# A fused decoder layer on one core: opening and closing written out, another standing order, gates as column tiles, three steps of each batch's negations on GpSimd

## Chip, cores and metric

One Trainium2 chip, one core. The metric is the device time of one execution in microseconds (us); the figure of a kernel is the median of its runs.

## What is computed

Sixteen independent batches of 256 rows by 256 columns in float32 go through one decoder layer:

```python
# per batch b, x[b] and ctx[b] are 256 x 256
x = layernorm(x + attn(x))                 # 16 heads of 16, scores + bias(|i-j|), softmax, Wo
x = layernorm(x + mlstm(x, ctx, ctx))      # 4 heads of 64: gates, cumulative sums, D matrix, head norm
x = layernorm(x + ffn(x))                  # 256 -> 1024 -> 256, rows quantised, weights ternary

# inside mlstm
ig = [q, ctx, ctx] @ igate_kernel + igate_bias          # 4 columns, fg alike
cs = cumsum(log_sigmoid(fg)); log_D = cs_i - cs_j + ig_j; m = max_j log_D
C = (q k^T / 8) * exp(log_D - m);  h = C v / (max(|sum C|, exp(-m)) + 1e-6)

# inside ffn
xq = round(x * 127 / max|row|);  wq = clip(round(w / mean|w|), -1, 1)
```

## The kernel before, in words

The work is written engine by engine. Each of the five blocks (SP for the DMAs, GpSimd, TensorE, ScalarE, VectorE) has a set of small functions, one for each step of a batch, and a function body(b) that calls them in an order written by hand. body(b) mixes four ages of batches: the projections of batch b+2, the attention of b and b+1, the memory part (gates, D matrix, values) of b-1 and b-2, and the feed-forward part of b-2 and b-3. body is called for b = -2 to B+3, and a step whose batch does not exist is left out (live). So the first and the last batches go through the same order as the middle ones, with holes.

Data passes between engines through semaphores. Each step waits until its inputs stand and until its output buffer is free, and an instruction that waits holds everything behind it on its engine.

For a group of the attention ("head" or step s), TensorE makes the scores (L599) into pS, VectorE adds the bias and takes the row maximum (L1292, two row tiles), ScalarE forms mx - score for row tile 0 (negated, L935) and GpSimd for tile 1 (negated, L437), TensorE transposes both tiles (turned, L615), ScalarE takes the exponential (L947), and TensorE multiplies four heads by their values in one call of values (L632). sc, pr and mx are rings of 8 heads.

The memory part: TensorE makes the gates in mem_gates with four matmuls that accumulate into one bank (L761 for the context, L764 for x1, 68 columns of which 8 are used). ScalarE reads them (L986 to L990), then takes the logarithm (L997, with a table load). VectorE sums (forget_sums, L1552), adds (input_rows, L1560), takes the running maximum (running_max, L1568), and a DMA writes this to DRAM (save_max, L319) and another one spreads it over all partitions (spread_max, L326). ScalarE takes its exponentials (mem_late, L966; mem_weights, L974), GpSimd masks (mem_causal, L489), VectorE multiplies (mem_weights, L1542), and TensorE makes the values (mem_values, L739 to L741).

The feed-forward part: rows are scaled on ScalarE (quantised, L1047), rounded back on VectorE (quantised_rows, L1467), turned on TensorE, multiplied (L693, L706), gated on VectorE, scaled on ScalarE (scaled, L1124), rounded back on GpSimd (inner_quantised, L449), turned by a DMA (turn_inner, L337), multiplied again (down, L751) and added to the residual (ffn_residual, L1532).

q and k are split into three bfloat16 parts on GpSimd (split_high and split_low, L414 to L427), and twelve DMAs of 128 KB a batch stack them (load_stack, L299).

All smaller products of TensorE share three PSUM banks, pA, pB and pC. The list uses fixes which name has which bank, by its place in the list modulo 3, and lease finds from the list whose release must be waited for. apart puts a semaphore increment of its own in front of some instructions.

Before the first body with scores stands a setup. All four attention weights are loaded and turned, the three bias vectors are spread by matmuls with a row of ones, the whole attention bias (4 MB) is loaded, and the three feed-forward weights are averaged (L1256), rounded (L1206, L1264, L1265) and turned on TensorE (L914) ahead of the iterations.

## Time and profile before

| | us |
|---|---|
| median of 3 runs | 768.72 |
| lowest and highest | 763.31 and 770.01 |
| the profiled execution, device time | 766.44 |
| its span in the profile | 764.6 |

The profile covers one execution. The span runs from its first to its last instruction; the device time is 1.8 us more. PE is TensorE's matmuls, PEld its weight loads, DVE VectorE, ACT ScalarE, POOL GpSimd, and SPq the queue of SP that issues the DMAs.

### The profile page before, as it was taken

To read this page: it belongs to the slowest core of one execution; us is meant where nothing else is said; L and a number is where in the kernel's file an instruction comes from. 1 tells how busy PE (TensorE), PEld (TensorE's weight loads), DVE (VectorE), ACT (ScalarE), POOL (GpSimd) and SP (SyncE) were. 2 spreads that over 40 slices of the span, in tenths; PEclk is the share of its full clock that TensorE was granted. 3 is DMA by queue.
4 is the path that set the end of the run, shared out by engine and by line. 5 is a ranking of instruction groups with operands and counts; after the bars stand their busy time and mean duration, and the time that the engine had idled before them with its cause. 6 is when DMAs were issued, how large, how long until landed. Compare 5 with 4: busy or idle time off the path is not lost.

```text
span 764.6 us, 17069 instructions
## 1 busy us (share of the span) xinstructions
PE 640.8 (84%) x4882; PEld 476.4 (62%) x4912; DVE 617.4 (81%) x2261; ACT 597.5 (78%) x1253; POOL 483.2 (63%) x833
## 2 busy tenths in 40 slices
PE   4367997999999999999999999989999989785542
PEld 3345776667676758686868676867676757452311
DVE  2755464899999999999999999988999999875752
ACT  0415795999999998989898999988999989875421
POOL 2415654667777868787778777776777765535332
PEclk8587998999999999999999999999999999897855
DMA  8887624154445545454545453635353542120201
GB/s 266 156 143 111 97 60 74 23 114 65 123 74 112 83 113 84 111 84 112 84 111 84 109 87 89 95 85 101 70 117 60 108 59 72 42 56 15 69 15 41
DMA packets 96966, 68.32 MB, mean 89 GB/s; under 512 B 40229, under 2 KB 96618, under 8 KB 96874
## 3 DMA queue, kind: packets, MB, share of 16 engines
q1 hardware_dynamic: 96874, 67.23, 44.7%
q8 instruction: 41, 0.67, 0.4%
q14 instruction: 51, 0.42, 0.2%
HBM read 29.39 MB, written 4.26 MB: 44 GB/s over the span
## 4 chain that ended last, share of the span: by engine, by line
PE 28%; DMA 23%; ACT 13%; SPq 10%; DVE 10%; issue 10%; POOL 6%; POOLq 0%; ACTq 0%; DVEq 0%
DMA mb<-mrows 13%; DMA th<-hq 7%; SPq L299 6%; PE pT L615 3%; PE pO L632 3%; ACT L997 2%; PE pA L751 2%; ACT h L1124 2%; SPq L337 2%; DVE mm L1568 2%; PE pB L739 2%; DMA ks<-parts 2%; PE pB L764 1%; PE pB L761 1%; PE pS L599 1%
## 5 line engine op out<-in xcount | busy, mean ns | idle before, releaser
L1292 DVE CUSTOM_DVE_ANT_0 sc<-pS,bias 128x256 f32<-128x256 f32 x512 | 201.4, 416 | 28.0 <-PE pS L599 26.8
L947 ACT ACTIVATE pr<-pT 128x512 f32<-128x512 f32 x256 | 154.5, 608 | 22.0 <-PE pT L615 21.4
L615 PE MATMUL pT<-ident,sc 128*128 128x128 f32 x1024 | 153.1, 277 | 5.1 <-POOL sc L437 3.2
L437 POOL TENSOR_SCALAR sc<-sc,mx 128x256 f32<-128x256 f32 x256 | 123.3, 493 | 23.3 <-DVE mx L1292 20.8
L615 PEld LDWEIGHTS pT<-ident,sc 128*128 128x128 f32 x1024 | 119.6, 142 | 28.1 <-issue 17.1
L935 ACT ACTIVATE sc<-sc,mx 128x256 f32<-128x256 f32 x256 | 130.2, 516 | 3.0 <-DVE mx L1292 3.0
L599 PE MATMUL pS<-ks,qs 96*128 96x256 bf16 x512 | 93.8, 274 | 9.1 <-DVE mx L1292 6.5
L489 POOL TENSOR_SCALAR_AFFINE_SELECT mb<-mb 128x256 f32<-128x256 f32 x64 | 26.3, 411 | 80.2 <-ACT mb L974 79.2
L632 PE MATMUL pO<-pr,va 128*32 128x256 f32 x1024 | 70.2, 393 | 0.5 <-ACT pr L947 0.5
L599 PEld LDWEIGHTS pS<-ks,qs 96*128 96x128 bf16 x512 | 47.9, 98 | 34.0 <-DVE mx L1292 17.0
L449 POOL TENSOR_SCALAR hq<-h 128x512 bf16<-128x512 f32 x64 | 38.7, 620 | 32.0 <-ACT h L1124 31.8
L414 POOL TENSOR_SCALAR parts<-qk_f 128x512 bf16<-128x512 f32 x32 | 19.9, 621 | 56.0 <-ACT qk_f L1092 39.1
L751 PE MATMUL pA<-wd,th 128*128 128x256 bf16 x256 | 37.4, 295 | 19.4 <-DMA th<-hq 17.8
L1036 ACT ACTIVATE x<-y,shift,rs 128x256 f32<-128x256 f32 x64 | 34.7, 592 | 20.3 <-POOL shift L402 20.3
L632 PEld LDWEIGHTS pO<-pr,va 128*32 128x32 f32 x1024 | 27.1, 110 | 29.8 <-issue 9.7
L1488 DVE TENSOR_TENSOR h<-h,pA 128x512 f32<-128x512 f32 x64 | 43.7, 683 | 1.1 <-PE pA L706 0.7
L1304 DVE BATCH_NORM_STATS2 st<-y 128x6 f32<-128x256 f32 x96 | 36.0, 417 | 9.4 <-POOL y L505 9.3
L751 PEld LDWEIGHTS pA<-wd,th 128*128 128x128 bf16 x256 | 25.4, 104 | 28.9 <-issue 22.6
L1124 ACT ACTIVATE h<-h,magic,hs 128x1024 f32<-128x1024 f32 x32 | 39.5, 1236 | 4.6 <-DVE hs L1521 4.6
L391 POOL TENSOR_SCALAR ve<-mv 128x2 f32<-128x2 f32 x48 | 12.2, 254 | 48.7 <-DVE mv L1314 48.5
L416 POOL TENSOR_TENSOR qk_f<-qk_f,parts 128x512 f32<-128x512 f32 x32 | 41.2, 1287 | 2.7
L1292 DVE DVE_READ_ACCUMULATOR2_ANT mx<- 128x1 f32 x512 | 41.5, 81 | 0.0
(223 smaller groups left out, 1736.3 us busy)
## 6 DMA issues: line engine op xcount, KB each, us to landing
qs<-parts SPq DMA_DIRECT2D x96, 128.0 KB, 4.7
ks<-parts SPq DMA_DIRECT2D x96, 128.0 KB, 4.5
mb<-mrows SPq DMA_DIRECT2D x16, 512.0 KB, 7.5
xin<-in_x SPq DMA_DIRECT2D x16, 256.0 KB, 2.8
bias<-in_L_attn_pos_bias SPq DMA_DIRECT2D x4, 1024.0 KB, 20.8
xb<-in_x SPq DMA_DIRECT2D x16, 256.0 KB, 3.0
cx<-in_ctx SPq DMA_DIRECT2D x32, 128.0 KB, 2.1
out<-hq SPq DMA_DIRECT2D x16, 256.0 KB, 3.2
```

Source lines behind the costliest of these rows:

```text
L299: sp.dma_start(dst, src).then_inc(stack.sem, 16)
L416: pool.tensor_tensor(src, src, parts[:, 0, which, :, :], ALU.subtract).then_inc(split.sem, 1)
L437: pool.tensor_scalar(sc[:, s % RING, 1, :], sc[:, s % RING, 1, :], -1.0, mx[:, s % RING, 1:2], ALU.mult, ALU.add).then_inc(neg_g.sem, 1)
L599: ins = pe.matmul(pS[s % 2][:, t * S:t * S + S], qs[par][:, s, t * P:t * P + P], ks[par][:, s, :], start=True, stop=True)
L615: ins = pe.transpose(bank[:, kt * S + t * P:kt * S + t * P + P], sc[:, s % RING, t, kt * P:kt * P + P], ident[:])
L632: ins = pe.matmul(pO[32 * j:32 * j + 32, 0:S], va[par][:, kt, hd, :], pr[:, hd % RING, kt, :], start=(kt == 0), stop=(kt == TT - 1))
L751: ins = pe.matmul(bank[:, 0:D], hqT[:, t, j, :], wd[:, j, :], start=(j == 0), stop=(j == FT - 1))
L935: act.activation(sc[:, s % RING, 0, :], sc[:, s % RING, 0, :], ACT.Identity, bias=mx[:, s % RING, 0:1], scale=-1.0).then_inc(neg_a.sem, 1)
L947: act.activation(flat(pr[:, s % RING, :, :]), pT[s % 2][:, :], ACT.Exp, scale=-1.0)\
L1124: act.activation(h[:, t, :], h[:, t, :], ACT.Identity, bias=magic[:, :], scale=hs[:, 4, t:t + 1])\
L1292: dve.tensor_tensor_reduce(out=sc[:, s % RING, t, :], in0=pS[s % 2][:, t * S:t * S + S], in1=bias[:, t, s, ::-1], scale=1.0, scalar=LOW, o ...
L1488: dve.tensor_tensor(dst, dst, bank_of(f"u{i}")[:, :], ALU.mult).then_inc(h_v.sem, 1)
```

## The change

- The bodies are called for batches 4 to 11 alone. opening() and closing() stand in each engine's block as lists of calls, each list with an order of its own, and body(b) has another order too.
- lease no longer reads a list of uses. TensorE's calls are counted as the program is built: each lease takes the next of the three banks and waits for the release, found in the table freed, of what held that bank. y0 and y1 of a batch had one bank and now have two.
- The setup is part of the opening. Loads have the order Wq, x[0], Wk, bq and bk, a quarter of the bias, Wv, x[1], the next quarter, Wo, the three spread bias vectors (by DMA), w_gate. The bias tile holds 384 columns for each head and the two row tiles read overlapping windows of it, 3 MB in place of 4. The feed-forward weights go one at a time through the tile h, and are turned by DMAs instead of TensorE. Their steps on ScalarE and VectorE lie between steps of batches 0 and 1, those of w_gate ahead of the first scores.
- k of batch 0 is split on VectorE.
- Gates: gate_parts makes four matmuls into four column tiles of 32, ScalarE copies the result (gate_copy), and gate_sums adds the four by one matmul with a matrix fold of zeros and ones.
- In heads 2, 7 and 12 of each batch GpSimd forms both row tiles of the negation, and ScalarE none.
- quantised_rows and input_rows go from VectorE to GpSimd.
- apart is gone.

```diff
+POOL_HEADS = (2, 7, 12)
-        bias = sb("bias", [P, TT, NH, S])
+        bias = sb("bias", [P, NH, S + P])
...
         def lease(eng, name, batch):
 
-            n = names.index(name)
...
+            if len(leases) >= len(shared):
+                other, n = leases[-len(shared)]
+                signal, k = freed[other]
+                eng.wait_ge(signal.sem, signal.at(n, k))
+            banks[name, batch] = shared[len(leases) % len(shared)]
+            leases.append((name, batch))
+            return banks[name, batch]
...
+            def gate_parts(c):
...
+                for j in range(4):
+                    rows = cxT if j < KT else x1T
+                    ins = pe.matmul(bank[32 * j:32 * j + 32, 0:S], gate_w[:, 2 + j if j < KT else j - KT, :],
+                                    rows[:, j % KT, :], start=True, stop=True)
+                ins.then_inc(gp_ps.sem, 1)
...
+                bank = lease(pe, "gates", c)
+                pe.wait_ge(gp_sb.sem, gp_sb.at(c, 1))
+                pe.matmul(bank[0:64 + XH, 0:S], fold[:, :], gt[:, :], start=True, stop=True).then_inc(gt_ps.sem, 1)
...
+            def weight_turn(i):
+                sp.wait_ge(wt_v.sem, 2 * i + 2)
...
+                sp.dma_start_transpose(dst, tern[i]).then_inc(d_wt[i].sem, 16)
...
-                pool.tensor_scalar(sc[:, s % RING, 1, :], sc[:, s % RING, 1, :], -1.0, mx[:, s % RING, 1:2],
-                                   ALU.mult, ALU.add).then_inc(neg_g.sem, 1)
+                for t in range(TT) if s in POOL_HEADS else (1,):
+                    ins = pool.tensor_scalar(sc[:, s % RING, t, :], sc[:, s % RING, t, :], -1.0, mx[:, s % RING, t:t + 1],
+                                             ALU.mult, ALU.add)
+                ins.then_inc(neg_g.sem, 1)
...
+                pool.tensor_scalar(xq[:], xr[:], 1.0, -MAGIC, ALU.mult, ALU.add).then_inc(xq_g.sem, 1)
...
+                pool.tensor_tensor(am[z, :], gt[z, :], cs[:, :], ALU.add).then_inc(am_g.sem, 1)
...
+            opening()
+            for b in range(FIRST, LAST):
+                body(b)
+            closing()
```

How the order moves, at three places. First TensorE in a middle batch, around the gates, before (L751 is down for row tile 1, L761 and L764 are the gates, L599 scores, L615 a transpose, L648 the projections of q and k, pS to pC the banks):

```order
L751 MATMUL pA<-wd,th 128x256 x8
L599 MATMUL pS<-ks,qs 128x256 x2
L615 MATMUL pT<-ident,sc 128x128 x4
L761 MATMUL pB<-cxT,gate_w 68x256 x2
L764 MATMUL pB<-x1T,gate_w 68x256 x2
L599 MATMUL pS<-ks,qs 128x256 x4
L648 MATMUL pC<-xT,wqT 128x256 x4
L599 MATMUL pS<-ks,qs 128x256 x2
L615 MATMUL pT<-ident,sc 128x128 x8
L585 MATMUL pA<-ident_b,xq 128x128 x4
L648 MATMUL pB<-xT,wkT 128x256 x4
L599 MATMUL pS<-ks,qs 128x256 x4
```

And in the changed kernel (L456 down, L470 gate_parts, L274 the transpose of x of batch b+2, L480 gate_sums, L290 scores, L308 transposes, L341 q and k):

```order
L456 MATMUL pB<-wd,th 128x256 x8
L470 MATMUL pC<-cxT,gate_w 32x256 x2
L470 MATMUL pC<-x1T,gate_w 32x256 x2
L274 MATMUL pA<-ident,xin 128x128 x4
L480 MATMUL pB<-gt,fold 68x256
L290 MATMUL pS<-ks,qs 128x256 x4
L308 MATMUL pT<-ident,sc 128x128 x8
L341 MATMUL pC<-xT,wqT 128x256 x4
L308 MATMUL pT<-ident,sc 128x128 x4
L290 MATMUL pS<-ks,qs 128x256 x2
L341 MATMUL pA<-xT,wkT 128x256 x4
```

The two pairs of gate matmuls become four narrow ones and a sum, with the transpose of x between them. The transposes of three heads, in place of two, stand between the gates and the projection of k, and the transpose of the quantised rows has moved behind k.

Second the DMAs of SP for a middle batch, before (L337 turns the quantised inner rows, L299 stacks q or k, L319 and L326 write and spread the running maximum, L342 stores, L312 loads the context, L305 and L331 load x):

```order
L337 DMA_TRANSPOSE th<-hq 128x8x128
L299 DMA ks<-parts 16x8x512 x6
L337 DMA_TRANSPOSE th<-hq 128x8x128
L319 DMA mrows<-mm 4x256
L305 DMA xin<-in_x 128x2x256
L331 DMA xb<-in_x 128x2x256
L326 DMA mb<-mrows 128x4x256
L299 DMA qs<-parts 16x8x512 x6
L342 DMA out<-hq 128x2x256
L312 DMA cx<-in_ctx 128x256 x2
```

And in the changed kernel (L1263 turns the inner rows, L1225 stacks, L1245 and L1252 write and spread the maximum, L1268 stores):

```order
L1263 DMA_TRANSPOSE th<-hq 128x8x128
L1231 DMA xin<-in_x 128x2x256
L1263 DMA_TRANSPOSE th<-hq 128x8x128
L1225 DMA ks<-parts 16x8x512 x6
L1245 DMA mrows<-mm 4x256
L1257 DMA xb<-in_x 128x2x256
L1252 DMA mb<-mrows 128x4x256
L1268 DMA out<-hq 128x2x256
L1225 DMA qs<-parts 16x8x512 x6
L1238 DMA cx<-in_ctx 128x256 x2
```

The six DMAs that stack k stood between the two transposes of a batch and now stand behind both. The load of x has gone from between the write and the spread of the maximum to between the two transposes.

Third the beginning of TensorE, before up to the first scores (L568 turns the attention weights, L573 to L578 spread the bias vectors, L902 averages and L914 turns the feed-forward weights, L672 is the projection of v):

```order
L578 MATMUL pT<-cxT,hq 128x1 x4
L585 MATMUL pA<-ident,xin 128x128 x4
L648 MATMUL pC<-xT,wqT 128x256 x4
L648 MATMUL pB<-xT,wkT 128x256 x4
L902 MATMUL pT<-w_abs,cxT 128x3
L914 MATMUL pO<-ident_b,h 128x128 x8
...
L585 MATMUL pA<-ident,xin 128x128 x4
L672 MATMUL pC<-wvT,xT 128x256 x4
L648 MATMUL pC<-xT,wqT 128x256 x4
L648 MATMUL pB<-xT,wkT 128x256 x4
L599 MATMUL pS<-ks,qs 128x256 x12
```

And in the changed kernel (L256 turns the attention weights, L266 averages w_gate, L369 is v, L290 the scores):

```order
L274 MATMUL pA<-ident,xin 128x128 x4
L256 MATMUL pS<-ident,pr 128x128 x4
L341 MATMUL pB<-xT,wqT 128x256 x4
...
L341 MATMUL pC<-xT,wkT 128x256 x4
L266 MATMUL pA<-w_abs,cx 64x1 x2
L256 MATMUL pT<-ident,pr 128x128 x2
L274 MATMUL pB<-ident,xin 128x128 x4
L256 MATMUL pT<-ident,pr 128x128 x2
L369 MATMUL pC<-wvT,xT 128x256 x4
L341 MATMUL pA<-xT,wqT 128x256 x4
L341 MATMUL pB<-xT,wkT 128x256 x4
L290 MATMUL pS<-ks,qs 128x256 x6
```

The transposes of the feed-forward weights and the spreading of bias vectors have left TensorE, v of batch 0 has moved ahead of q and k of batch 1, and the average of w_gate has stayed ahead of the first scores.

## Rows read from the trace of the kernel before

**Rows 1.** The page, part 1: busy time, share and instructions of each engine

```profile
PE 640.8 (84%) x4882; PEld 476.4 (62%) x4912; DVE 617.4 (81%) x2261; ACT 597.5 (78%) x1253; POOL 483.2 (63%) x833
```

**Rows 2.** Stretches between the first scores, gates 0, 2, 12, 15 and the end

```profile
core 0: us, PE busy (x) PEld busy (x) DVE busy (x) ACT busy (x) POOL busy (x), PEclk, DMA share, GB/s
0.00:54.90 54.90, 25.77 (x128) 21.71 (x129) 28.93 (x38) 11.41 (x14) 13.83 (x25) 0.75 0.90 197
54.90:103.40 48.50, 41.67 (x312) 31.44 (x313) 25.25 (x127) 32.22 (x71) 30.34 (x50) 0.89 0.56 82
103.40:184.20 80.80, 72.22 (x567) 55.65 (x567) 60.73 (x247) 67.34 (x147) 49.98 (x82) 0.96 0.42 80
184.20:582.00 397.80, 376.33 (x3003) 285.12 (x3022) 367.95 (x1391) 366.22 (x780) 298.13 (x511) 1.00 0.48 94
582.00:698.40 116.40, 99.38 (x767) 70.32 (x770) 98.82 (x363) 96.30 (x202) 71.94 (x131) 0.96 0.28 62
698.40:764.60 66.20, 25.48 (x112) 12.12 (x114) 35.75 (x96) 24.00 (x42) 18.95 (x37) 0.64 0.15 36
```

**Rows 3.** Timeline, 0 to 60 us (start, us, engine, line; idle before in brackets)

```profile
9.16 0.81 DVE L1234 COPY hq<-th 1x256 f32<-1x256 f32 x2 [9.16 <-DMA gate_b<-in_L_xattn_fgate_bias]
...
21.08 4.61 DVE L1256 TENSOR_REDUCE w_abs<-sc 128x1 f32<-128x2048 f32 x2
...
22.99 3.78 PE L648 MATMUL pC<-xT,wqT 128*128 128x256 f32 x8 [0.77 <-ACT xT L1083]
...
31.81 7.31 SPq L299 DMA_DIRECT2D qs<-parts  x6
...
32.45 2.01 POOL L416 TENSOR_TENSOR qk_f<-qk_f,parts 128x512 f32<-128x512 f32 x1
...
54.90 0.61 PE L599 MATMUL pS<-ks,qs 96*128 96x256 bf16 x4 [0.31 <-DMA ks<-parts]
```

**Rows 4.** The chain that ended last, 262 to 302 us (start, us, what)

```profile
269.24 0.99 DVE mm L1568
...
271.62 8.16 DMA mb<-mrows
...
282.19 0.46 PE pA L739 x2
...
290.85 0.59 SPq L299
...
294.75 5.27 DMA th<-hq
```

**Rows 5.** Timeline of TensorE, middle batches (181 to 190 and 262 to 302 us)

```profile
182.40 1.03 PE L761 MATMUL pB<-cxT,gate_w 128*68 128x256 f32 x4
...
184.12 0.60 PE L599 MATMUL pS<-ks,qs 96*128 96x256 bf16 x4
...
270.47 1.07 PE L632 MATMUL pO<-pr,va 128*32 128x256 f32 x16
271.47 0.66 PE L615 MATMUL pT<-ident,sc 128*128 128x128 f32 x4
...
282.19 0.46 PE L739 MATMUL pA<-cx,cT 128*128 128x128 f32 x2 [1.30 <-DVE cT L1542]
```

**Rows 6.** Groups of instructions, 262.45 to 421.32 us, four batches (busy us, mean ns)

```profile
L935 ACT ACTIVATE sc<-sc,mx 128x256 f32<-128x256 f32 x64 | 32.8, 519 | 0.0
L957 ACT ACTIVATE oT<-pO 128x256 f32<-128x256 f32 x16 | 6.3, 392 | 1.2 <-PE pO L632 1.2
L437 POOL TENSOR_SCALAR sc<-sc,mx 128x256 f32<-128x256 f32 x64 | 30.9, 494 | 1.9 <-DVE mx L1292 1.1
L1292 DVE CUSTOM_DVE_ANT_0 sc<-pS,bias 128x256 f32<-128x256 f32 x129 | 51.3, 415 | 1.0 <-PE pS L599 0.5
L1467 DVE TENSOR_SCALAR xq<-att 128x512 bf16<-128x512 f32 x4 | 2.6, 662 | 0.6 <-ACT att L1047 0.4
L1560 DVE TENSOR_TENSOR am<-gt,cs 4x256 f32<-4x256 f32 x4 | 1.6, 412 | 0.1
```

More of the change, by code:

```diff
@@ L224, in lease @@
         def lease(eng, name, batch):
-            n = names.index(name)
-            it = batch + uses[n][1]
-            for back in range(1, 2 * len(uses)):
-                i, m = (it, n - back) if back <= n else (it - 1, n - back + len(uses))
-                if m < 0:
-                    break
-                other, behind, freed, k = uses[m]
-                if bank_of(other) is bank_of(name) and live(i - behind):
-                    wait(eng, freed, i - behind, k)
-                    break
@@ L608, in turned @@
                 bank = pT[s % 2]
-                pe.wait_ge(neg_a.sem, lin + 1)
+                act_heads = s + 1 - sum(h <= s for h in POOL_HEADS)
+                if s not in POOL_HEADS:
+                    pe.wait_ge(neg_a.sem, neg_a.at(b, act_heads))
                 pe.wait_ge(neg_g.sem, lin + 1)
@@ new lines, in body @@
+                down(e, 0)
+                turned(b, 5)
+                v_proj(n)
+                scores(b, 10, par)
+                x1_turned(c, 1 - par)
+                down(e, 1)
+                gate_parts(c)
+                x_turned(n2, par)
+                gate_sums(c)
+                scores(b, 11, par)
+                scores(b, 12, par)
+                turned(b, 6)
+                turned(b, 7)
+                q_proj(n2)
+                turned(b, 8)
+                scores(b, 13, par)
@@ L917, in _ @@
-            pe.wait_ge(v_set.sem, V_ALL)
-            iterations(pe, body)
+                mem_scores(c, 0)
+                scores(n, 5, 1 - par)
+                turned(b, 14)
+                turned(b, 15)
+                mem_values(c, 0)
+                mem_scores(c, 1)
+                scores(n, 6, 1 - par)
+                mem_values(c, 1)
+                values(b, 3, par)
+                mem_values(c, 2)
+                heads_turned(b, 0)
+                heads_turned(b, 1)
+                turned(n, 0)
@@ L1211, in _ @@
+            act.wait_ge(g_set.sem, G_ALL)
+            opening()
+            for b in range(FIRST, LAST):
+                body(b)
+            closing()
         @block.vector
@@ L1706 @@
+            opening()
+            for b in range(FIRST, LAST):
+                body(b)
+            closing()
 _INS = ["x", "ctx_1024", "L0_attn_Wq", "L0_attn_bq", "L0_attn_Wk", "L0_attn_bk", "L0_attn_Wv", "L0_attn_bv",
```

3340 lines of the change are left out of this document (2749 added, 591 removed).

## The prediction

> **What bounds the kernel now.** I read the busy shares first, then the stretches, then the chain of waits, then TensorE's timeline. The shares name no single bound: TensorE 84%, VectorE 81%, ScalarE 78%, GpSimd 63% [rows 1]. The stretches show why. I cut the span at the first scores (54.9 us) and where the gates of batches 0, 2, 12 and 15 end [rows 2]. To the first scores go 54.9 us with TensorE busy for 25.8. From gates 2 to gates 12 ten batches take 397.8, so 39.8 each, and in each TensorE is busy 37.6, VectorE 36.8, ScalarE 36.6, GpSimd 29.8. The last three batches take 38.8 each, and behind gates 15 come 66.2 us in which no engine is busy for more than 54%: a chain of latencies. So there are three prices: the start, the batch, the end.
>
> In a middle batch three engines have 2 to 3 us of air each, and no more than one loop of waits fits in. The chain [rows 4] shows that loop: gates, running maximum at 269.24, the DMA that spreads it (8.16 us), values of the memory at 282.19; then the inner rows, whose turning DMA takes 5.27 and stands behind six issues of k's stack at 0.59 (some 3.8 us with gaps), then down and the next gates. TensorE's own row shows the price: it stood 1.30 us in front of the values, for cT [rows 5]. Relieving one engine by 1 us therefore gives 1 us at most, and only if the loop gets shorter too.
>
> **The batch.** Gates: from 182.40 to the scores at 184.12 TensorE spent 1.72 us on the four products of L761 and L764 with 256 columns, 0.43 each [rows 5]. Four heads' values, eight products in column tiles 32 wide, took 270.47 to 271.47, 1.00, so four such take 0.50. With gate_sums (0.43) the new gates cost 0.93 and save 0.79. In the 1.00 us a switch of tile width is already contained: eight products at 0.43, four at a time, would be 0.86. If the 0.14 belongs to each visit and not to each product, gate_parts costs 0.57, and the saving is 0.72. The Trainium skill has the rule behind this (TensorEngine Tiling (Array Packing), Key Properties: "Mode switching requires drain"); by it the change adds one such visit a batch, and the sum is 0.07 us a batch worse, 1 us in all. The row agrees in size.
>
> ScalarE: three negations at 0.519 leave, the copy of the gates (shape of L957, 0.392) comes: 1.17 less; records of ScalarE overlap, so I count 1.0 [rows 6]. VectorE: 0.662 and 0.412 leave, 1.07 less [rows 6]. GpSimd: three negations at 0.494, quantised_rows and input_rows come. Neither has a row on GpSimd. The first has 512 columns, so it lies between one L437 and two, 0.49 to 0.99; the second has 256 columns on 4 partitions, from 0 (if only partitions counted) to 0.49. I take 0.65 and 0.4: 2.5 more, 32.3 in a batch. The removed apart increments have no row. They take nothing at least, and on VectorE, with 16 a batch, at most its 3 us of idle time [rows 2]; that time is explained by waits, so I count nothing.
>
> So work per batch becomes TensorE 36.8, VectorE 35.7, ScalarE 35.6, GpSimd 32.3. Keeping the air of before (2.2, 3.0, 3.2) gives 38.7 to 39.0.
>
> The order says whether the loop allows it. From the end of the gates (184.12, or 263.4 in the batch of rows 4) to the memory's values at 282.19 went 18.8 us, with 15.7 of work on TensorE. In the new order this stretch holds two more scores (0.22 each), two more heads' transposes (0.44) and one more call of values (1.00): 18.0. Its chain grows as well: one exponential ahead of the logarithm (about 0.5, as L935), four VectorE tiles ahead of the running maximum (0.415 in the record and some 0.35 from start to start, 1.4), one tanh between the two exponentials of the mask (0.5) [rows 6]. The step on GpSimd lies beside the four tiles, and the load of x leaves the place in front of the spread (0.4 less). Some 2.1 in all, so 20.9 to 21.2. The other stretch, values to gates, loses these 2.3 and the gates' 0.8 from its 21.0: 17.9. Its DMA wait should go, because k's stack no longer stands between the two turnings, 3.8 us of slack for the second. Sum 38.8 to 39.1. With the 38.7 to 39.0 above I take 38.8, 1.0 less than now. From gates 2 to 12: 10.0 us gained. For the last three intervals, 38.8 now and bound more by latency, I take half, 0.6 each: 1.8.
>
> New waits in this order: gate_sums waits for ScalarE's copy, with 0.44 of transposes as cover; the copy's 0.39 and two hops may leave 0.2 uncovered, and behind it stand two scores, which VectorE has waiting. Heads 2, 7, 12 are negated in 0.99 instead of two engines' 0.5; the ring of eight hides that. input_rows on GpSimd can stand behind a negation (0.5); the four VectorE tiles cover it.
>
> **The start.** Now VectorE does nothing until 9.16, when the last small load lands, q of batch 0 is projected at 22.99, the stack's DMAs are issued from 31.81 over 7.3 us and land only shortly before 54.90, behind 4 MB of bias [rows 3]. Meanwhile VectorE averages (4.61 for two weights) and rounds all three weights. In the new order q needs x[0] and Wq alone, the first loads. My steps, estimates built on these rows: q projected from 8; k done by 15.5; both copied by 17.5; GpSimd splits q by 22 (1.16 to 2.01 for one of its four steps [rows 3]); SP issues both stacks in 7.5 at the pace of rows 4, to 29.5; landing by 33.5. The other branch: w_gate's average 2.3, its rounding on ScalarE and VectorE about 4.7, v of batch 0, then x, q and k of batch 1 are all ahead of the first scores and end at about 33 too. I take 33.5, a gain of 21.4. Bounds: 28 if TensorE runs at 2.4 GHz (now 0.75 granted here [rows 2]) and the queue is empty; 45 if the 4.5 MB issued before the stacks delay them as the bias does now.
>
> From the first scores to gates 0 there are 48.5 now. The new order reaches gates 0 with one head's scores and three heads' transposes fewer and without x, q and k of batch 1: 4.3 less on TensorE; w_up's steps (about 5 on VectorE, 2 on ScalarE) hide, as these engines are busy 25 and 32 of 48.5 [rows 2], and may cost 1.3 where the queue is in order. So 45.5, a gain of 3.0. From gates 0 to 2 there are 80.8, though the feed-forward part is empty in most of it; a list of its own can close these holes. TensorE has 72.2 of work there, less 1.6 for gates; w_down and two transposing DMAs of 512 KB lie in it. I take 74, a gain of 6.8 (bounds 0 and 9). The 16 copies and turns of the old setup are paid in the start already.
>
> **The end.** Behind gates 15 the chain is the same: it gains the copy (0.4) and loses the wait of y1 for y0's bank (0.5, an estimate by L957's like shape). 66.2 stays, -1 to +2.
>
> **The sum.** 21.4 + 3.0 + 6.8 + 10.0 + 1.8 = 43.0 from the profiled execution's 766.4 gives 723.4. The median of the runs lies 2.3 above that execution, so 726.
>
> **Rivals.** (a) The batch keeps its 39.8. The stretches' sum is only as good as my chain: if the memory chain grows by 2.1 and the other stretch cannot go below 19, what TensorE gains is idled away at cT. For it speaks the 1.30 us wait that the engines' shares don't show, against it the six stack issues that leave the second transposition. Only start and early batches stay: 768.7 - 31.2 = 738. (b) The loop closes better than now: cT's 1.3 us goes, batches take 38.0, and the ends written apart are planned tighter, 3 us: 726 - 10.4 - 3 = 713. VectorE and ScalarE would be 94% busy; now they are at 92%, so it is possible. (c) The start does less than it says, because w_gate's steps and its DMA stand ahead of the first scores on three engines: scores at 45 and the batch as forecast: 737.5. (d) Slower. GpSimd becomes the bound. One row shows the mechanism: L416 took 2.01 at 32.45, against its usual 1.16, while VectorE ran through a 2048-column tile [rows 3]. GpSimd has seven two-input steps of 512 columns a batch; if each took 0.85 more, its 32.3 would be 38.3, and with the 3 us or more that it waits for other engines in any order, a batch takes 42. That is 2.2 more than now, 33 over 15 intervals, against 31 gained at the edges (start, early batches): 771. From 1.0 us for each step on it decides. Against it: in middle batches GpSimd's sum of 29.8 is made of the short durations, and one VectorE step of the disturbing kind leaves. The Trainium skill states the cause (GPSIMD Engine Reference, Specifications: SBUF interfaces shared with VectorE); the trace of one stretch agrees, the middle batches hardly.
>
> **Chances.** Forecast 0.52, (a) 0.20, (b) 0.15, (c) 0.10, (d) 0.03. The forecast's own bounds come from the start (28 to 40) and the batch (38.4 to 39.2, over 13 intervals 5 each way): 716 to 735. To hold 8 in 10 the range takes in (a), (c) and most of (b): 709 to 744. A measurement of this kernel tells about 1% from no change, 761 to 776; only a mix of (a), (c) and (d) comes there. Faster 0.96, same 0.02, slower 0.02.
>
> **What would show it.** First scores near 33.5, gates 0 near 79, gates 2 near 153. Middle batches at 38.8, TensorE busy 36.8, GpSimd 32.3. The wait for cT in front of the memory's values stays at about 3 us less what other waits take, and the wait for the turned inner rows is gone. Gate work on TensorE 0.93 in two pieces. Behind gates 15 some 66 us. The forecast is wrong if middle batches stay above 39.5, or if the first scores come after 42.

## The result

| | before | after |
|---|---|---|
| median of 4 runs, us | 769.15 | 737.79 |
| lowest and highest | 763.31 and 770.01 | 735.66 and 739.16 |
| the profiled execution's span | 764.6 | 736.1 |

The ratio is 0.9605 (0.9552 to 0.9658): 4.0% faster. The forecast was 726 with a range of 709 to 744. The likeliest case was 12 us too low, and the figure of rival (a), 738, is the one that came, though not by (a)'s way.

The page of the changed kernel, part 1, answers [rows 1]: TensorE has 18 us less work, VectorE 34 and ScalarE 15 less, GpSimd 43 more.

```profile
PE 622.3 (85%) x4862; PEld 453.5 (62%) x4892; DVE 583.5 (79%) x2227; ACT 582.9 (79%) x1221; POOL 526.1 (71%) x909
```

The stretches, cut at the same events as [rows 2] (columns as there):

```profile
0.00:36.20 36.20, 20.42 (x68) 15.73 (x69) 12.72 (x19) 6.15 (x8) 8.19 (x21) 0.76 0.92 186
36.20:80.80 44.60, 37.15 (x298) 26.65 (x296) 33.24 (x135) 32.06 (x65) 31.45 (x50) 1.00 0.93 169
80.80:160.00 79.20, 72.08 (x589) 54.34 (x590) 60.05 (x244) 67.55 (x149) 58.51 (x94) 0.98 0.54 92
160.00:549.90 389.90, 369.02 (x3000) 275.20 (x3020) 345.60 (x1368) 354.76 (x756) 325.03 (x558) 1.00 0.55 97
549.90:672.20 122.30, 99.55 (x802) 69.51 (x808) 98.28 (x369) 97.28 (x204) 80.57 (x145) 0.97 0.29 59
672.20:736.10 63.90, 24.11 (x113) 12.10 (x114) 33.65 (x97) 25.10 (x43) 22.38 (x43) 0.67 0.15 37
```

| stretch | before | after | change | predicted |
|---|---|---|---|---|
| to the first scores | 54.9 | 36.2 | -18.7 | -21.4 |
| to gates 0 | 48.5 | 44.6 | -3.9 | -3.0 |
| gates 0 to 2 | 80.8 | 79.2 | -1.6 | -6.8 |
| gates 2 to 12 | 397.8 | 389.9 | -7.9 | -10.0 |
| gates 12 to 15 | 116.4 | 122.3 | +5.9 | -1.8 |
| behind gates 15 | 66.2 | 63.9 | -2.3 | 0 |
| sum | 764.6 | 736.1 | -28.5 | -43.0 |

So the start and the middle are near what was said. Two terms are missing: gates 0 to 2, and the last three intervals, which became longer. The end of the last gates matmul of each batch, read from TensorE's timeline, gives the intervals (us). Some of the cuts above lie up to 0.6 us beside these ends; by the ends the last three changes of the table are -7.3, +5.8 and -2.8:

```
            0-1  1-2  2-3  3-4 ... 10-11 11-12 12-13 13-14 14-15  behind
before      40.0 41.0 39.3 39.7    40.0  39.5  39.8  36.7  39.4   66.7
after       33.6 45.7 37.8 38.9    39.1  41.4  42.5  40.8  38.4   63.9
```

Eight bodies in the middle (gates 3 to 11) took 318.9 before and 311.4 after: 39.9 and 38.9 each. TensorE's waits in these stretches tell what changed. First the two largest of before (engine, line, waited for: us in total, times, longest):

```profile
PE pA L739 <- DVE cT L1542: 6.1, 8, 1.3
PE pA L751 <- DMA th<-hq: 3.9, 7, 1.6
```

and the two largest of the changed kernel:

```profile
PE pS L290 <- DVE mx L2807: 9.1, 16, 0.9
PE pA L274 <- ACT x L2009: 1.2, 2, 0.7
```

The wait of [rows 5] for cT is gone as well as the one for the turned rows, and TensorE now stands in front of scores (L290), for VectorE's row maximum (L2807). The spread of the running maximum (8.16 us in [rows 4]) lands in 4.5 us in the median, from 7.5 before.

### The profile page after: what moved, and what is told of

Read it like the earlier page. It is cut to its first block, busy times and chain, and to the rows that moved or that the text cites. A ratio compares the mean times of both kernels' runs of the same rounds, so it can differ in the third digit from the quotient of the medians.

```text
span 736.1 us, 16566 instructions
## 1 busy us (share of the span) xinstructions
PE 622.3 (85%) x4862; PEld 453.5 (62%) x4892; DVE 583.5 (79%) x2227; ACT 582.9 (79%) x1221; POOL 526.1 (71%) x909
## 4 chain that ended last, share of the span: by engine, by line
PE 42%; POOL 12%; ACT 12%; issue 12%; DVE 11%; DMA 3%; POOLq 0%; SPq 0%; DVEq 0%; ACTq 0%
PE pT L308 8%; PE pO L325 5%; PE pS L290 4%; DVE sc L2807 3%; POOL nrm L1501 2%; ACT L1970 2%; POOL rs L1416 2%; ACT x L2009 2%; POOL sc L1453 1%; DMA cx<-in_ctx 1%; DVE mm L3067 1%; DMA mb<-mrows 1%; PE pC L409 1%; PE pA L274 1%; PE pA L394 1%
## 5 line engine op out<-in xcount | busy, mean ns | idle before, releaser
L2807 DVE CUSTOM_DVE_ANT_0 sc<-pS,bias 128x256 f32<-128x256 f32 x512 | 198.3, 416 | 25.3 <-PE pS L290 23.2
L1453 POOL TENSOR_SCALAR sc<-sc,mx 128x256 f32<-128x256 f32 x304 | 150.1, 504 | 35.1 <-DVE mx L2807 33.7
L308 PE MATMUL pT<-ident,sc 128*128 128x128 f32 x1024 | 146.7, 275 | 6.5 <-ACT sc L1898 2.4
L308 PEld LDWEIGHTS pT<-ident,sc 128*128 128x128 f32 x1024 | 117.5, 141 | 24.5 <-issue 9.7
L290 PE MATMUL pS<-ks,qs 96*128 96x256 bf16 x512 | 95.4, 275 | 18.4 <-DVE mx L2807 17.7
L1898 ACT ACTIVATE sc<-sc,mx 128x256 f32<-128x256 f32 x208 | 102.3, 513 | 8.2 <-DVE mx L2807 8.2
L290 PEld LDWEIGHTS pS<-ks,qs 96*128 96x128 bf16 x512 | 43.2, 98 | 54.5 <-DVE mx L2807 34.4
L2109 ACT ACTIVATE h<-h,magic,hs 128x1024 f32<-128x1024 f32 x32 | 39.7, 1239 | 4.0 <-DVE hs L3027 4.0
L2807 DVE DVE_READ_ACCUMULATOR2_ANT mx<- 128x1 f32 x512 | 42.3, 83 | 0.0
L3002 DVE TENSOR_REDUCE hs<-h 128x1 f32<-128x1024 f32 x32 | 38.8, 1213 | 0.4 <-issue 0.2
L1433 POOL TENSOR_TENSOR qk_f<-qk_f,parts 128x512 f32<-128x512 f32 x31 | 36.0, 1161 | 2.6
L1443 POOL TENSOR_TENSOR parts<-qk_f,parts 128x512 bf16<-128x512 f32 x31 | 36.0, 1161 | 2.6
L1416 POOL TENSOR_TENSOR rs<-ve,minus_half 128x2 f32<-128x2 f32 x48 | 34.9, 727 | 1.3
L1937 ACT ACTIVATE mb<-mb,aT 128x256 f32<-128x256 f32 x64 | 33.4, 521 | 0.4
```

Source lines behind the costliest of these rows:

```text
L290: ins = pe.matmul(pS[s % 2][:, t * S:t * S + S], qs[par][:, s, t * P:t * P + P], ks[par][:, s, :], start=True, stop=True)
L308: ins = pe.transpose(bank[:, kt * S + t * P:kt * S + t * P + P], sc[:, s % RING, t, kt * P:kt * P + P], ident[:])
L1416: pool.tensor_tensor(rs[:, which, :], ve[:, which, :], minus_half[:, 0:TT], ALU.pow)\
L1453: ins = pool.tensor_scalar(sc[:, s % RING, t, :], sc[:, s % RING, t, :], -1.0, mx[:, s % RING, t:t + 1], ALU.mult, ALU.add)
L1898: act.activation(sc[:, s % RING, 0, :], sc[:, s % RING, 0, :], ACT.Identity, bias=mx[:, s % RING, 0:1], scale=-1.0).then_inc(neg_a.sem, 1)
L2109: act.activation(h[:, t, :], h[:, t, :], ACT.Identity, bias=magic[:, :], scale=hs[:, 4, t:t + 1])\
```

## The experiments

Twelve kernels ran. Ratios are to the kernel before, run on the same chip (its median was 764.8 to 766.3 there, and 769.15 where the changed kernel ran), so kernels of different chips are compared by their ratios. All compute the whole layer.

The last column is the mean of the eight intervals from gates 3 to 11.

| | median us | ratio (95%) | middle batch us |
|---|---|---|---|
| before | 769.15 | 1 | 39.9 |
| changed kernel | 737.79 | 0.9605 (0.9552 to 0.9658) | 38.9 |
| e1_swap | 738.19 | 0.9625 (0.9579 to 0.9672) | 38.9 |
| e2_close | 735.11 | 0.9587 (0.9531 to 0.9644) | 38.9 |
| e3_neg_act | 748.44 | 0.9769 (0.9728 to 0.9810) | 40.2 |
| e4_gates_wide | 741.27 | 0.9686 (0.9640 to 0.9733) | 39.3 |
| e5_late | 750.31 | 0.9777 (0.9693 to 0.9861) | 38.9 |
| e6_rows_dve | 747.86 | 0.9756 (0.9693 to 0.9820) | 39.7 |
| e7_before_heads | 768.18 | 1.0029 (0.9998 to 1.0059) | 39.9 |
| e8_before_sp | 746.52 | 0.9747 (0.9677 to 0.9817) | 38.5 |
| e9_before_qs | 756.93 | 0.9910 (0.9871 to 0.9949) | 39.2 |
| e10_sp_old | 772.65 | 1.0103 (1.0051 to 1.0155) | 43.0 |
| e11_mended | 735.12 | 0.9613 (0.9578 to 0.9648) | 38.8 |
| e12_mended2 | 735.08 | 0.9607 (0.9563 to 0.9652) | 38.8 |

### SP's queue: e8, e9, e10

e8_before_sp gives the kernel before the changed kernel's order in SP's queue, and nothing else:

```diff
+                load_x(n2, par)
                 turn_inner(d, 1)
+                load_stack(b, par, 1)
                 save_max(f)
-                load_x(n2, par)
                 load_residual(c)
                 spread_max(f)
-                load_stack(n, 1 - par, 0)
                 store(d)
+                load_stack(n, 1 - par, 0)
                 load_ctx(c)
                 turn_inner(e, 0)
-                load_stack(n, 1 - par, 1)
```

> The kernel before with the order of SP's queue as in the changed kernel's middle batch: both transposes of the inner rows ahead of the stack of k, the load of x ahead of the second, q's stack behind the store. Computes the same. Theory A (the wait of ScalarE for the spread maximum, 11.7 us in 14 batches, was a term of the middle batch, and comes from the stack of k in front of the write and the spread): the landing goes from 7.5 to 4.5 us, the wait to under 2 in all, the batch from 39.8 to 39.3 or less, 756 to 762. Theory B (the wait goes but something else is just as late): the wait goes and the batch stays 39.7 to 39.9, 764 to 768. That the stack of k comes too late for the scores of its batch would show as 40 and more.

746.52, some 19 us less than before on the same chip, from ten calls in another order. That is more than theory A asked for. The landing of the spread maximum fell from 7.5 to 4.8 us in the median, and the batch became 38.5, shorter than the changed kernel's 38.9. What is left in the list of TensorE's waits in eight batches:

```profile
PE pB L693 <- ACT qk_f L1103: 4.1, 8, 0.5
PE pC L693 <- issue: 1.3, 7, 0.2
PE pA L585 <- DVE xq L1467: 0.2, 1, 0.2
```

TensorE's work stayed (300.2 us in eight batches, 301.0 before), only its idle time went, from 17.9 to 7.5.

e9_before_qs takes one half of this edit, q's stack behind the store; k's stack stays between the two transposes.

```diff
                 spread_max(f)
-                load_stack(n, 1 - par, 0)
                 store(d)
+                load_stack(n, 1 - par, 0)
```

> The kernel before with one edit in SP's queue: the stack of q goes behind the store instead of ahead of it, so that it no longer follows 1.7 us behind the spread of the maximum. The stack of k stays between the two transposes. Computes the same. SP's whole order of the changed kernel took before to 746.5 and the batch from 39.8 to 38.45, and TensorE's waits for cT (6.1 us in eight batches) and for th (3.9) both went. Theory A (the spread maximum that landed in 7.5 us beside the stack of q was the larger part): landing 4.8, the wait for cT gone, that for th still there, the batch 38.7 to 39.2, 750 to 757. Theory B (the transpose behind the stack of k was what counted, the spread hidden): the batch 39.5 or more, 762 or more.

756.93, a batch of 39.2. The landing was 5.1, and the wait for cT is gone from the list while that for the turned rows stands (before: 3.9):

```profile
PE pA L751 <- DMA th<-hq: 4.2, 7, 1.8
```

So of 1.4 us a batch about half (0.7) belongs to the spread maximum that q's stack followed. The other half is what is left over: TensorE's wait for the turned rows, 4.2 us in eight batches here and none in e8, is 0.5 of it. No run moved k's stack alone, and e8 moves the load of x as well, which was not run by itself.

e9's trace shows the spread's price twice. In its first two batches, where there is no store yet, q's stack is still issued 1.70 and 1.64 us behind the spread, and the spread lands in 7.67 and 6.26 us; in the others it is issued 7.5 us or more behind, or not at all, and the spread lands in 4.1 to 5.6.

e10_sp_old does the reverse: the changed kernel with the old places of the two stacks in its eight middle bodies.

```diff
                 load_x(n, 1 - par)
-                turn_inner(d, 1)
                 load_stack(b, par, 1)
+                turn_inner(d, 1)
                 save_max(f)
                 load_residual(c)
                 spread_max(f)
-                store(d)
                 load_stack(n, 1 - par, 0)
+                store(d)
```

> The changed kernel with SP's queue in the eight middle bodies as before: the stack of k ahead of the second transpose of the inner rows, the stack of q straight behind the spread of the maximum. Computes the same. Theory A (this order is what made the middle batch of the changed kernel shorter, whatever the other engines' orders): the batch goes from 38.9 to 39.8 or more in eight batches, 745 to 750. Theory B (the order of TensorE in the changed kernel, with the transposes of three heads behind the gates, hides both landings): 38.9 to 39.2, 737 to 741.

772.65: 35 us are gone, and the changed kernel would be 1% slower than the one before (1.0103, 1.0051 to 1.0155). Seven intervals, from gates 2 to gates 9, are 42.7 to 44.7; the mean in the table has two of 39.2 in it that the edit doesn't reach, and without them it is 44.2. SP's queue in one of them (start, us, DMA):

```profile
319.31 1.29 SPq L1263 DMA_TRANSPOSE th<-hq  x1
320.71 0.53 SPq L1231 DMA_DIRECT2D xin<-in_x  x1
321.28 3.83 SPq L1225 DMA_DIRECT2D ks<-parts  x6
325.21 1.32 SPq L1263 DMA_TRANSPOSE th<-hq  x1
```

The second transpose is issued 5.9 us behind the first. TensorE's waits in the stretch 197.8 to 509.2:

```profile
PE pA L456 <- DMA th<-hq: 8.8, 3, 3.2
PE pS L290 <- DVE mx L2807: 8.6, 14, 1.0
PE pC L456 <- DMA th<-hq: 7.9, 4, 3.7
PE pB L456 <- DMA th<-hq: 6.7, 2, 3.4
```

The landing of the spread maximum stayed at 4.7, so here all of it is the transpose. It stayed although q's stack is again the next call behind the spread, because SP must wait for q's parts from GpSimd. SP's queue shows it (start, us, DMA), before:

```profile
271.62 0.42 SPq L326 DMA_DIRECT2D mb<-mrows  x1
273.29 3.78 SPq L299 DMA_DIRECT2D qs<-parts  x6
```

and in e10:

```profile
300.54 0.37 SPq L1252 DMA_DIRECT2D mb<-mrows  x1
308.31 3.81 SPq L1225 DMA_DIRECT2D qs<-parts  x6
```

In the changed kernel the first issue of q's stack comes 7.8 us behind the spread too. So there the orders of the other engines alone keep the two apart, and the new place of q's stack counts only in the old kernel (e8, e9). In the changed order down stands straight ahead of the gates; where down waits 3 us for its rows, the gates of the next batch wait too, and the loop gets longer by more than the wait. The changed orders of the other four engines need this order of SP more than the old ones did.

### The three heads on GpSimd: e3, e7

e3_neg_act returns the negations of heads 2, 7 and 12 to ScalarE (the waits follow):

```diff
-POOL_HEADS = (2, 7, 12)
+POOL_HEADS = ()
...
+                if s in (3, 8, 13):
+                    negated(b, s - 1)
```

> Heads 2, 7 and 12 have their row tile 0 negated on ScalarE again, next to the negation of heads 3, 8 and 13; all else as in the changed kernel. Theory A (the batch is set by what the three busy engines must do): ScalarE gets 1.2 to 1.5 us back in a batch, 35.6 to 37.0, and middle batches go from 38.9 to 39.7 to 40.2, in all +12 to +18, near 752. Theory B (the batch is set by the loop of waits over the maximum's DMA, and ScalarE has air): under +0.3 a batch, under +5, near 740.

748.44; the batch became 40.2, and the new wait is one of TensorE for ScalarE's negation, 1.1 us in each batch:

```profile
PE pT L308 <- ACT sc L1900: 8.7, 8, 1.1
```

The place of the three negations, next to those of heads 3, 8 and 13, is mine. An earlier place might cost less, as e8 negates row tile 0 of all heads on ScalarE and keeps a batch of 38.5; so the 1.3 holds for this order, and bounds the worth of the three heads from above.

e7_before_heads does this part alone on the kernel before:

```diff
+POOL_HEADS = (2, 7, 12)
...
+                for t in range(TT) if s in POOL_HEADS else (1,):
+                    ins = pool.tensor_scalar(sc[:, s % RING, t, :], sc[:, s % RING, t, :], -1.0, mx[:, s % RING, t:t + 1],
```

> The kernel before with heads 2, 7 and 12 of row tile 0 negated on GpSimd, nothing else. Computes the same. In the changed kernel taking these three back to ScalarE cost 1.3 us in each middle batch (40.2 for 38.9) and 10.7 us in all. Theory A (the three steps are the main gain of the middle batch, in either order): the batch goes from 39.8 to 38.5 to 39.0, the time 766 to about 750. Theory B (the order before is bound elsewhere, by the wait for the spread maximum, 7.5 us from issue to landing, or by VectorE at 36.8 us a batch; the steps pay only with the new order): 39.6 to 39.9, 762 to 769.

768.18, ratio 1.0029: nothing. Eight batches of it, gates 3 to 11:

```profile
220.80:539.60 318.80, 300.86 (x2402) 228.43 (x2417) 295.07 (x1111) 284.00 (x601) 248.59 (x432) 1.00 0.49 94
```

ScalarE has 9 us less to do than before's 293.0 and GpSimd 10 more, in 318.8 us against 318.9. The work left ScalarE and the loop stayed; with e8 beside it, that loop ran through SP's queue.

### The two steps moved from VectorE: e6

```diff
-                pool.tensor_tensor(am[z, :], gt[z, :], cs[:, :], ALU.add).then_inc(am_g.sem, 1)
...
             def running_max(c):
+                dve.tensor_tensor(am[z, :], gt[z, :], cs[:, :], ALU.add).then_inc(am_g.sem, 1)
...
+                rows_rounded(c - 1)
```

> The changed kernel with input_rows and quantised_rows back on VectorE, around the running maximum. Computes the same. VectorE gets 0.2 + 0.6 us a batch more, GpSimd 0.6 + 0.6 less. Theory A (the shift to GpSimd relieved VectorE, the batch is bound by all engines in turn): the batch goes from 38.9 to 39.2 or more, 742 to 748. Theory B (the two hops to GpSimd lie in the chain gates, sums, input rows, running maximum, and lengthen it): the batch goes to 38.5 to 38.8, 731 to 737. A waiting quantised_rows may also hold VectorE where ScalarE's scaling is late, which would speak for A.

747.86, a batch of 39.7 (gates 3 to 11). VectorE's work in eight batches rose from 277.0 to 280.8, 0.5 us a batch, so 0.3 of the 0.7 us are more than the work; two of the eight intervals, 40.6 and 40.5 among others of 39.3 to 39.4, hold most of that. The place behind the running maximum is mine and not the one of the kernel before, so this bounds the shift's worth from above.

### The gates: e4

e4_gates_wide makes the gates again with four accumulating products at gate_sums' place, and ScalarE copies nothing.

```diff
-                    ins = pe.matmul(bank[32 * j:32 * j + 32, 0:S], ..., start=True, stop=True)
+                    ins = pe.matmul(bank[0:64 + XH, 0:S], ..., start=(j == 0), stop=(j == 3))
```

> The gates are four accumulating products with 68 columns again, at the place of gate_sums; no gate_parts, no copy on ScalarE. Theory A (TensorE's work counts): TensorE +0.79 a batch, ScalarE -0.4, middle batches 38.9 to 39.5, in all +8 to +12, near 748. Theory B (what counts is the loop of waits, in which the copy and the two pieces stand as well): the loop loses about as much as it gains, -0.3 to +0.3 a batch, 734 to 742.

741.27, inside theory B's 734 to 742, while the batch's 0.4 lies between the two theories. TensorE's work rose by 0.6 us a batch (301.1 in eight for 296.3), the batch by 0.4. The changed kernel's own gates on TensorE:

```profile
312.50 0.41 PE L470 MATMUL pB<-cxT,gate_w 128*32 128x256 f32 x2
...
313.07 0.66 PE L274 MATMUL pC<-ident,xin 128*128 128x128 f32 x4
313.73 0.62 PE L480 MATMUL pA<-gt,fold 128*68 128x256 f32 x2
314.19 0.60 PE L290 MATMUL pS<-ks,qs 96*128 96x256 bf16 x4
```

gate_parts takes 312.50 to 313.07, 0.57, and gate_sums 0.46: 1.03 for 1.72 before. Four narrow products take more than half of what eight take in [rows 5], so the 0.14 belongs to each visit. That is the second of the two readings that the prediction weighed, the one that the Trainium skill's rule points to (TensorEngine Tiling (Array Packing), Key Properties), and the trace agrees with it in size: 0.57 against 0.50 without it. What the 0.14 consists of no run here shows.

### The start: e5

e5_late puts the average and the rounding of w_gate behind the first scores. In the changed kernel the start looks like this:

```profile
20.90 2.29 DVE L2769 TENSOR_REDUCE w_abs<-h 128x1 f32<-128x2048 f32 x1 [1.97 <-DMA h<-in_L_ffn_w_gate]
...
24.27 3.85 SPq L1225 DMA_DIRECT2D ks<-parts  x6
...
30.70 3.75 PE L341 MATMUL pA<-xT,wqT 128*128 128x256 f32 x8 [0.84 <-ACT xT L2056]
...
36.32 0.60 PE L290 MATMUL pS<-ks,qs 96*128 96x256 bf16 x4
```

```diff
                 k_proj(0)
-                weight_mean(0)
                 weight_turned(6)
...
                 scores(0, 4, 0)
+                weight_mean(0)
                 scores(0, 5, 0)
...
-                weight_load(1)
                 load_bias(2)
                 load_bias(3)
+                weight_load(1)
```

> The changed kernel with the average, rounding and copies of w_gate behind the first scores (its bias quarters are loaded ahead of w_up). Computes the same. In the changed kernel the first scores begin at 36.3 us, and TensorE stood idle 9.06 us ahead of the average of w_gate at 23.29. Theory A (w_gate ahead of the scores is what makes the start late): the first scores come by 32 to 34, gates 0 by 2 to 4 earlier, the time 734 to 736. Theory B (the stacks of q and k, which landed at about 36 in two of the experiments before, or the bias, bound the start): scores at 36, and nothing gained; if the w_gate work then lies in batch 0 where VectorE and ScalarE are busy, gates 0 come later, 738 to 742.

The first scores came no earlier, at 36.7, now behind a wait for the stack alone:

```profile
36.70 1.01 PE L290 MATMUL pS<-ks,qs 96*128 96x256 bf16 x4 [7.38 <-DMA ks<-parts]
```

k's stack was issued from 25.52 to 29.4 here, and the scores began 7.3 us behind the last issue. In e2 and e3, where q and k of batch 1 came a little sooner, the first scores waited 2.15 and 1.89 us for the stack too, to 36.20 and 35.85. Gates 0 came at 95.9 instead of 80.4, since w_up, loaded last, arrived late: VectorE waited 9.1 us for it at 57.26. k's stack was issued 1.25 us later here than in the changed kernel, so w_gate's work can have cost about 1 us of the start at most (an estimate: 36.70 less 1.25 is 35.4). Theory B holds within that. In the changed kernel's own trace two things end within 1 us: k's stack lands at 35.3, 7.2 us behind its last issue, and TensorE's chain of v, q and k, with no wait for the stack, ends at 36.3. The granted clock had gone to 0.50 (the 1.2 GHz level) while TensorE stood still for 9.06 us ahead of 23.29, and q, at 30.70, still ran at it and took 3.75 us. In e2, after a stand of 8.10, it was back at 1.00 from 30 us on (2.4 GHz), q took 1.96, k ended at 34.05, and the stack was what came last. The loss behind the first scores belongs to my place for w_up.

### The closing: e1, e2

e1_swap exchanges two calls on GpSimd where opening and closing have them in the other order than the body:

```diff
-                quantised_rows(12)
                 input_rows(13)
+                quantised_rows(12)
```

> GpSimd's order alone: in the written opening (batch 0/1) and closing (12/13, 13/14, 14/15) input_rows stands ahead of quantised_rows, as in the standing body; nothing else moves. Theory A (the slow intervals come from input_rows queued behind quantised_rows, which waits up to 3.6 us for ScalarE): the gates 1 to 2 interval falls from 45.7 to about 42, those after batch 12 by 1 to 2 each, in all 5 to 8 us, near 731. Theory B (the written orders cost by their whole arrangement, not by this pair): under 2 us, near 737.

738.19, and the closing's intervals are 41.3, 42.5, 41.9 and 38.3: nothing. The interval gates 1 to 2 is 40.4 in this trace, for 45.7, as theory A said, but that need not be the swap: e3 and e4, which leave the pair as it was, have 40.8. The profiled execution took 734.46, the other three of e1 737.69 to 738.77. So the short interval seems to come and go between executions of one kernel; that isn't shown, as each kernel has one trace.

e2_close leaves out the closing's lists and lets the body run to B + 3, as the kernel before did.

```diff
-            for b in range(FIRST, LAST):
+            for b in range(FIRST, B + 4):
                 body(b)
-            closing()
```

> The written closing is replaced on all five engines by the standing body, called to the end with holes, as the kernel before does; opening and body unchanged. Theory A (the written closing lists are what makes batches 11 to 13 take 41.1, 42.7 and 40.9 instead of 38.9): these intervals fall to 38.9, 38.9 and about 37, 8 to 10 us, and the stretch behind gates 15 goes from 63.9 to at most the 66.2 of before, so 729 to 732. Theory B (the draining itself costs this, as fewer batches overlap, and the list is the best that can be had): 738 or slower.

735.11. The four intervals from gates 11 to 15 are 38.8, 38.9, 39.6 and 40.7, in sum 158.0 for 163.1; behind gates 15 follow 66.2 for 63.9. So the closing's own order costs 5.1 and gives 2.3 back. The three intervals from gates 12 on are 119.1 here, 121.7 in the changed kernel and 115.9 before: 3.2 us of the loss stay with the ordinary body. The interval that lost most against before is the one from gates 13 to 14 (593 to 634 us), 40.8 for 36.7. In it ScalarE's mask exponentials come late and GpSimd waits, and the scores wait for the maximum; in e2's 39.6 these waits are 2.7 and 2.9:

```profile
POOL mb L1521 <- ACT mb L1937: 7.7, 3, 7.0
...
PE pS L290 <- DVE mx L2807: 3.6, 4, 2.3
```

### Gates 1 to 2, and a mended kernel: e11, e12

In the changed kernel's chain between gates 1 and 2 (start, us, what) stands a spread maximum that takes 8.66 us:

```profile
122.11 1.89 DVE mm L3067
124.02 1.25 DMA mrows<-mm
125.28 8.66 DMA mb<-mrows
```

In three kernels (the changed one, e2, e10) this spread landed in 8.6 to 8.8 us, and the interval was 45.2 to 45.7. In five (e1, e3, e4, e5, e6) it landed in 3.9 to 5.4, and the interval was 40.4 to 42.7, though none of the edits touches SP's queue around it. q's stack of batch 4 follows 2.4 to 3.7 us behind it. e11_mended moves that stack, calls the body for the closing, and moves two row maxima ahead of the gates' sums on VectorE:

```diff
-                load_stack(4, 0, 0)
                 load_ctx(2)
+                load_stack(4, 0, 0)
                 turn_inner(0, 0)
...
-                row_moments(e, 2)
-                forget_sums(c)
                 biased(b, 13, 1)
+                row_moments(e, 2)
+                forget_sums(c)
...
-                running_max(c)
                 biased(b, 15, 1)
+                running_max(c)
```

> The changed kernel with three edits, each to be read in its own stretch. (1) The closing by the middle body: 39.2, 38.9, 38.8, 39.6, 40.7 for the last five intervals, as in the experiment with it alone. (2) In the opening the stack of q of batch 4 behind the load of the context of batch 2, so that it doesn't follow 2.4 us behind the spread maximum of batch 1, which landed in 8.7 us twice where the interval gates 1 to 2 took over 45 us, and in 5.4 or less where it took 40.4 to 40.8: theory A the interval is 40 to 41; theory B (the landing is slow for another reason) it can still be 45. (3) On VectorE in the body, head 13's second row tile ahead of forget_sums and head 15's ahead of running_max, since TensorE's scores waited 9.1 us in eight batches for these two row maxima: theory A the batch goes from 38.9 to 38.0 to 38.5; theory B (the sums and the maximum come 0.4 to 0.8 later and take it back) 38.8 to 39.2. Computes the same. All A: 724 to 731; (1) alone as before: 735.

735.12. The spread never took more than 5.4 us, but the interval was 46.3, with another wait:

```profile
PE pB L456 <- DMA th<-hq: 4.0, 1, 4.0
```

SP issued the transpose at 147.45, behind 4.00 us of q's stack from 143.35: I had made in the opening what e10 makes in the body. The batch went from 38.9 to 38.8 only. TensorE's wait for the row maximum fell from 9.1 to 3.0 us in eight batches, and one for the exponentials of 4.6 took its place.

e12_mended2 puts the stack behind both transposes:

```diff
                 turn_inner(d, 1)
+                if b == FIRST:
+                    load_stack(b, par, 0)
                 load_stack(b, par, 1)
```

> As e11_mended, but the stack of q of batch 4 goes behind both transposes of batch 0's inner rows, just ahead of the stack of k, instead of ahead of them. In e11_mended the spread maximum of batch 1 landed in time (5.4 us or less) and TensorE did not stand still until 147 us, but the transposes of batch 0, now behind 4.0 us of q's stack, landed 5 us late, and gates 1 to 2 took 46.3. Computes the same. Theory A (the two waits, for the spread behind which q's stack follows and for the transposes behind it, are all that makes the interval 45 and more): gates 1 to 2 take 40 to 41, the rest as in e11_mended, the time 728 to 731. Theory B (the interval is bound by a chain through ScalarE and GpSimd as well, 4.0 us of DMA being only what came last): 42 to 44, 731 to 734. If q's stack now comes too late for the scores of batch 4, gates 3 come late: 39.5 or more for the next interval.

Gates 1 to 2: 40.2, as theory A says. But the next interval was 44.0 for 37.8, because batch 4's scores waited 5.1 us for their stack; this had been named as the risk. The time is 735.08, above the figures of both theories. By their ratios, 0.9613 and 0.9607, neither mended kernel can be told from the changed one at 0.9605. No version that beats it is shown. No run joined the old body with SP's new order (e8) to the new opening either. e8's gates 0 end at 101.8 and the changed kernel's at 80.7; 746.5 less these 21.1 would be 725, an estimate.

## Why the prediction was right, and where not

**The start** (said 21.4, came 18.7). That the small loads, 4 MB of bias and the setup leave the front is right. Scores came at 36.3 for 33.5, because k's stack, issued from 24.27 over 3.85 us, lands at 35.3, with the DMA engines busy for 0.92 of the stretch, and because TensorE's chain, at the 1.2 GHz level in its last part, ends no sooner than 36.3. I had let the stack land 4 us behind the last issue; it took 7.2 here and 7.3 in e5. To gates 0: 3.9 for 3.0, right.

**Gates 0 to 2** (said 6.8, came 1.6). "A list of its own can close these holes" was right for the first interval, 33.6, and in the traces where the spread of batch 1 landed in 3.9 to 4.8 us also for the second: e1, e3 and e4 have 40.4 to 40.8, so 73.9 to 75.3 for both, against the 74 that I said. The failed step is that the term held no spread that lands late: at 8.66 us, beside q's stack of batch 4, the interval is 45.7. TensorE stood 1.91 us in it and then ran a part at the lower clock. e12, with the stack elsewhere, has 40.2.

**The middle** (said 39.8 to 38.8, came 38.9 for the eight bodies; most of what the stretch to gates 12 lacks is the closing's first interval, 41.4). Size right, reason half right, so the size is in part luck. The sum by work (GpSimd 32.3, measured 32.7; VectorE 35.7, measured 34.6; TensorE 36.8, measured 37.0; ScalarE 35.6, measured 35.7) held. But "relieving one engine gives 1 us at most, and only if the loop gets shorter too" was the part that decides, and I put the whole gain on both. e8 shows that SP's order alone takes 1.4 us off the old batch with no work removed, e7 that the three heads alone take off nothing, and e10 that without SP's order the new ones lose 5.3 in the intervals that it reaches. The forecast that the wait for the turned rows goes, since k's stack leaves the place between the transposes, is shown by e10. The forecast that the wait for cT stays was wrong: q's stack 1.7 us behind the spread had made it slow (e9), and in the changed kernel the stack comes 7.8 us behind it. I had read the move in SP's rows only for k's stack and the load of x, and had not followed when q's parts are ready. Against e8's 38.5 the rest of the change costs 0.5 us a batch, in the new wait for row maxima, and in this kernel it needs the three heads (e3: 1.3), the column tiles (e4: 0.4) and the moved steps (e6: 0.7 at most) to stay there, each at the place that I gave it. The removed increments of apart and the second bank for y0 and y1 had no run of their own.

The sizes of GpSimd's new steps, in the groups of four batches (236.2 to 391.8 us), answer to [rows 6]:

```profile
L1453 POOL TENSOR_SCALAR sc<-sc,mx 128x256 f32<-128x256 f32 x76 | 37.1, 498 | 0.4
...
L1898 ACT ACTIVATE sc<-sc,mx 128x256 f32<-128x256 f32 x52 | 26.0, 516 | 0.2 <-DVE mx L2807 0.2
...
L1513 POOL TENSOR_TENSOR am<-gt,cs 4x256 f32<-4x256 f32 x4 | 2.9, 716 | 9.4 <-DVE cs L3059 9.4
L1463 POOL TENSOR_SCALAR xq<-att 128x512 bf16<-128x512 f32 x4 | 2.5, 617 | 1.7 <-ACT att L2020 1.7
```

quantised_rows took 0.62 (0.65 said), input_rows 0.72, outside the bounds of 0 to 0.49 that I had given it.

**The last three intervals** (said -1.8, came +5.9). I took half of the middle's gain for a stretch whose order I had not followed. e2 shows 5.1 us of cost in the closing's lists over four intervals, of which 2.6 fall into these three; 3.2 more stay with the ordinary body, and their cause is open. **The end** (said 0, came -2.3): the closing gives that back, as e2 without it has 66.2.

**The sum of the bounds.** By its own terms the narrow range is 715 to 738 (726 less 5.5 and 5.2, 726 plus 6.5 and 5.2), not 716 to 735. The 737.8 lies at its upper end, though the terms behind it are others than the two that this range was made of: the start and the batch came near, gates 0 to 2 and the closing did not.

**The rivals.** (a) said that the batch keeps 39.8: it didn't. (b)'s tighter ends went the other way. (c) came in part, by 2.7 us and by the stack rather than by w_gate. (d), GpSimd as the bound, is not seen: its negations took 0.498 for 0.494, and the splitting step that the rival was built on took 1.16 in the median from gates 2 to 12, for 1.28 before. Its busy share is 71%.

## What to carry to other kernels

Read the queue that issues the DMAs as an engine with a price: six issues of 0.6 us in front of a transpose that the longest loop waits for cost 5.3 us a batch here (e10). Move a small urgent transfer ahead of a bulk one before taking work off the compute engines, and test the two apart: the same three negations were worth nothing in the old order (e7) and up to 1.3 us a batch in the new one (e3). An order written out by hand for the last batches should be timed against the ordinary body run with holes.

## What was not expected of the hardware

An addition of 4 x 256 elements took 0.716 us on GpSimd and 0.412 on VectorE [rows 6], and the negation of 128 x 256 took 0.498 on GpSimd: four partitions didn't make it cheap.

The 512 KB spread of a maximum landed in 3.5 to 5.2 us in fifteen batches of the changed kernel and in 8.66 in one, with q's six issues 2.4 us behind its own. In e3 and e5 the same 2.4 us gave 3.90 and 5.40, so the distance alone doesn't decide; what does stays open.

A short stand was followed by a lower clock. In the changed kernel TensorE stood 1.91 us ahead of 135.78 and 0.65 ahead of 137.03. The granted clock was 1.00 up to 136, 0.50 from 138 to 140 (the 1.2 GHz level), and 1.00 again from 142 on. From one pair of L442 or L443 to the next it took 0.43 us at 138.11 to 139.82 and 0.22 from 143.65 on, at 2.4 GHz. The mean of 134 to 144 is 0.83, so the lower clock cost about 1.7 us (an estimate: 0.17 of 10 us) on top of the stand. In e1, without such a stand, it is 1.00 from 113.5 to 153.9.
